# A decoder layer on one core: ScalarE's table set with both logarithm and exponential, read in by the program itself

## What is computed

```python
x = x + attn(layernorm(x))       # 16 heads of 32, windows of 128 stepped by 64
x = x + wkv(w, u, layernorm(x), ctx_2048)
x = x + ffn(layernorm(x))        # 512 -> 2048 -> 512, weights and activations rounded
```

## Time and profile before

| | |
|---|---|
| median of 3 runs | 1103.22 us (1102.84 to 1103.45) |
| the profiled execution, own time | 1107.51 us |
| its span, first to last instruction | 1106.2 us |
| TensorE (PE) busy | 860.3 us, 78% |
| VectorE (DVE) busy | 848.1 us, 77% |
| ScalarE (ACT) busy | 706.9 us, 64% |
| GpSimd (POOL) busy | 436.7 us, 39% |
| mean granted TensorE clock | 0.924 of 2.4 GHz |

### The profile page before, as it was taken

How to read it: one execution, slowest core, us unless ns; L and a number is a source line. 1 busy time by engine, 2 the same in 40 slices (tenths; PEclk the granted TensorE clock), 3 DMA queues, 4 the chain that set the end, 5 groups by cost and what they waited for, 6 DMA issues and landing times.

```text
span 1106.2 us, 21992 instructions
## 1 busy us (share of the span) xinstructions
PE 860.3 (78%) x8301; PEld 512.9 (46%) x8388; DVE 848.1 (77%) x1630; ACT 706.9 (64%) x1179; POOL 436.7 (39%) x495
## 2 busy tenths in 40 slices
PE   5782565768888889897988888888888888986655
PEld 2341444444455555555545555555555554543222
DVE  4552659798888888888888888888788888887953
ACT  0113838077777777777768686868586868594633
POOL 2110113225353535353535354544444444445532
PEclk9896786769999999999999999999999999998978
DMA  8867516011524252525242424243342525122132
GB/s 293 288 217 277 188 58 189 10 59 36 93 68 83 78 83 78 84 78 83 79 83 78 80 82 77 85 75 87 62 99 58 104 58 103 49 78 29 39 58 66
DMA packets 148762, 106.93 MB, mean 97 GB/s; under 512 B 99792, under 2 KB 126128, under 8 KB 147504
## 3 DMA queue, kind: packets, MB, share of 16 engines
q1 hardware_dynamic: 142128, 101.48, 36.2%
q0 software_dynamic: 656, 2.63, 0.7%
q10 hardware_dynamic: 5872, 1.42, 0.6%
HBM read 65.65 MB, written 10.49 MB: 69 GB/s over the span
## 4 chain that ended last, share of the span: by engine, by line
ACT 31%; PE 23%; DVE 18%; issue 15%; DMA 3%; SPq 2%; POOL 1%; DVEq 0%; ACTq 0%; POOLq 0%
PE bank L494 9%; ACT arena L722 6%; PE bank L593 5%; PE bank L513 5%; ACT L774 3%; ACT sums L729 3%; DVE junk L1146 3%; PE bank L583 2%; ACT sums L734 2%; ACT junk L774 2%; ACT junk L779 2%; DVE amax L1112 2%; DVE fs L1155 2%; ACT L745 2%; ACT L722 2%
## 5 line engine op out<-in xcount | busy, mean ns | idle before, releaser
L583 PE MATMUL bank<-w_up_gate,qT 128*128 128x512 bf16 x966 | 232.5, 386 | 48.4 <-ACT junk L774 24.1
L1350 POOL TENSOR_TENSOR work<-junk,lnw 128x512 f32<-128x512 f32 x128 | 188.2, 1490 | 125.1 <-DVE junk L1146 110.7
L1333 POOL TENSOR_TENSOR sums<-sums,blend 128x448 f32<-128x448 f32 x64 | 73.2, 1163 | 270.5 <-ACT sums L734 270.5
L583 PEld LDWEIGHTS bank<-w_up_gate,qT 128*128 128x128 bf16 x1024 | 96.5, 99 | 155.3 <-ACT junk L774 26.9
L593 PE MATMUL bank<-w_down,work 128*128 128x512 bf16 x483 | 125.6, 408 | 25.3 <-ACT junk L774 10.6
L494 PE MATMUL bank<-wide,wq_sb 128*128 128x256 f32 x512 | 117.7, 389 | 27.7 <-DVE rows L1047 27.7
L513 PE MATMUL bank<-wide,k_win 32*128 32x128 f32 x1536 | 70.5, 320 | 82.2 <-ACT arena L722 54.2
L722 ACT ACTIVATE arena<-bank 128x384 f32<-128x384 f32 x256 | 104.8, 496 | 36.7 <-PE bank L513 36.6
L494 PEld LDWEIGHTS bank<-wide,wq_sb 128*128 128x128 f32 x512 | 98.3, 195 | 53.1 <-issue 39.7
L774 ACT ACTIVATE junk<-bank,deq 128x512 f32<-128x512 f32 x128 | 86.3, 686 | 52.5 <-PE bank L583 50.7
L545 PE MATMUL bank<-wo_sb,wide 128*128 128x512 f32 x256 | 115.9, 607 | 4.1 <-DVE wide L1040 4.1
(11 more groups left out here) (150 smaller groups left out, 1541.2 us busy)
## 6 DMA issues: line engine op xcount, KB each, us to landing
rows<-in_x SPq DMA_DIRECT2D x24, 512.0 KB, 5.4
sums<-in_xT SPq DMA_DIRECT2D x16, 512.0 KB, 8.8
wide<-in_xT SPq DMA_DIRECT2D x16, 512.0 KB, 4.2
ctx_T<-in_ctxT SPq DMA_DIRECT2D x16, 512.0 KB, 4.0
wide<-wide SPq DMA_DIRECT2D x64, 128.0 KB, 2.1
out<-rows SPq DMA_DIRECT2D x32, 256.0 KB, 2.2
kv_b<-k_raw SPq DMA_DIRECT2D x16, 384.0 KB
wide<-in_x SPq DMA_DIRECT2D x8, 512.0 KB, 9.3
```

What stands on the lines that cost most here:

```text
L583: last = te.matmul(bank[4 + k % 4][:, :], qT[:, c, t * P:(t + 1) * P], w_up_gate[:, m, c, cols], start=c == 0, stop=c == NC - 1)
L1350: ge.tensor_tensor(hid_w[:, t, cols], hid[:, n % 2, :], lnw[:, cols], op=ALU.mult).then_inc(z_set.sem, 1)
```

## The change

A function `log_tables` is added to ScalarE's stream. It issues one InstLoadActFuncSet for set 6, which holds both Ln and Exp. It is called twice a round where there is a wkv stage (rounds 1 to 16): ahead of `exps(w)` and ahead of `wkv_logs(w, 0)`. The compiler's pass then places no load where the active set already has the function. Nothing else moves, and what is computed stays the same.

```diff
+LN_EXP = 6
...
+        def log_tables():
+            se.add_instruction(mybir.InstLoadActFuncSet(name=nc.get_next_instruction_name(),
+                                                        engine=mybir.EngineType.Activation, act_func_set_id=LN_EXP))
+
...
             if do_w:
+                log_tables()
                 exps(w)
...
             if do_w:
+                log_tables()
                 wkv_logs(w, 0)
```

## The result

| | before | changed |
|---|---|---|
| median of the runs, us | 1103.03 (1102.05 to 1103.45) | 1121.21 (1120.43 to 1122.51) |
| ratio, 95% interval | 1 | 1.0156 [1.0134, 1.0178] |
| profiled execution, us (span) | 1107.51 (1106.2) | 1121.32 (1119.7) |
| loads of a table set | 129 | 84 |
| ScalarE busy, us | 706.9 | 645.9 |

The account below looks back on a forecast made before the run. No engine alone bounds the kernel; the chain goes round between engines (ScalarE 31%, TensorE 23%, VectorE 18%). Steady rounds cost 7.7 + 2.6 = 10.3, i=1 and i=16 give 2.6: 1103.2 + 7.7 = 1111 us, range 1088 to 1117 (own 1103 to 1117).

Parts of the forecast that it names:

- The turns: VectorE and GpSimd instructions on SBUF would meet and wait for each other; L1090 0.7 us late at full clock.
- the tie: First L1040 of VectorE (590.95) against GpSimd's L1370 (590.94); if L1040 wins, the round is 0.0 to 0.1 late, not 0.7.
- A round's price: Full-clock round 0.7 us late if L1370 goes first, 0.0 to 0.1 if L1040 does; with TensorE's clock fallen, 1.1 late.
- Seven rounds with a fall x 1.1 = 7.7: Seven rounds in which TensorE's clock falls to 1.2 GHz for a few microseconds, each 1.1 us late: 7.7 us slower.
- one in every round adds 10: Bound: a fall of TensorE's clock in every round adds 7 x (1.0 + 0.4) = 10 us; given 0.05.
- The first rounds: Round i=1, three loads in its chain: between 0 and 3.9 us off, 2.3 taken.
- The anchor: Profiled execution 1107.51 would take 1115.2; the median of runs is 4.3 below it, so 1103.2 + 7.7 = 1111 us.
- Rival 1: Faster: VectorE-GpSimd meetings cost little and TensorE's 1.3 us gap closes; 1079, or 1092 with half eaten; chance 0.30.
- its point of decision: If a round's last L1040 (VectorE) ends before GpSimd's L1350 behind the third blend starts, the round keeps its lead.
- Rival 2: No difference: the tie goes to VectorE everywhere and clock falls are no more; 1101 to 1105 us; chance 0.14.
- Rival 3: A load costs more than its row by emptying ScalarE: 1.4 us by the rows; 983 us has chance below 0.01.
- Rival 4: The automatic load still follows a set read in by the program, so the time stays as now; chance 0.01.

Follow-up runs that it names:

- experiment 6: Changed kernel with all three removed loads of a round put back where they stood, each loading the set already there: 0.9997 of the kernel before.
- experiment 3: Changed kernel with GpSimd's first product of the second token half (L1359) held for the previous round's quotient, long done: 1.0120 of the kernel before.
- the seventh experiment: Changed kernel with the third load kept (ahead of the exponentials of quarters 2 and 3) and window sums from PSUM: 0.9822 of the kernel before, 1085.78 us.
- the three fillings: 13 idle matmuls in TensorE's waits (1.05, 1.97, 1.3 us), added to kernel before, changed kernel and fastest version: 0.9962, 1.0013, 0.9764 of the kernel before.
- the fourth experiment: Changed kernel with weighted window products left in PSUM and their halves added by one reduce with a single PSUM input: 0.9951 of the kernel before, 1099.21 us.

## Why the prediction was off

The direction and its mechanism were right, the size was not: 1121.2 is 10 above the forecast and 4 above the range.

- **What the loads give.** Right: 84 loads; the third logarithm 2.83 nearer to the second and the exponentials 2.93 (forecast 2.8 and 3.0); TensorE's wait for the Silu gone.
- **The turns.** Right, nearly place by place: the tie went to L1379; L1092 1.62, L1099 1.68 (1.3 to 1.7 were named, but only one of each pair meets, so their medians are 1.16 and 1.18); L1379 1.64; the last L1049 0.94 (0.9 to 1.2); the second L1099 13.08 behind the second logarithm (12.5 to 13.3). The rule that the Trainium skill gives (SBUF — State Buffer, Who interferes with whom) held in its direction in every round read here. An L1049 of 0.36 that lay across a L1359 ended 0.21 behind it, so some 0.15 of it had overlapped; "fully blocks" alone would have given 0.36.
- **A round's price.** At full clock 0.53 against 0.7 (tie lost) or 0.05 (won); I took the middle, 0.37. With a fall 57.7 to 57.9 against 56.7, 1.0 to 1.2, as forecast.
- **The term that was mis-sized: "Seven rounds with a fall x 1.1 = 7.7".** It took the number of falls over from one execution of the kernel before and held it constant under the change; only the price of a turn was added. What the twelve rounds i=3 to 14 hold above twelve full-clock rounds (12 x 55.70 or 12 x 56.23) is the falls' share:

| | rounds with a fall | above full clock, us |
|---|---|---|
| kernel before, first and second profile | 7, 6 | 9.2, 6.6 |
| all loads back (experiment 6) | 5 | 7.4 |
| changed kernel, first and second profile | 7, 9 | 10.9, 15.6 |
| its hold that held nothing (experiment 3) | 7 | 12.4 |

In the first pair of profiles the twelve rounds grew by 8.0 us (685.61 - 677.59), near the forecast (12 of 14 rounds, 8.8). But that execution of the kernel before was 4.3 above its median and held eight falls; the forecast took off the 4.3 and kept the falls. Against the second profile of before (1103.10), the span of the changed kernel's first is 17.9 longer: 6.4 by turns and 4.3 by falls in the twelve rounds, 2.5 in i=2, 3.2 in i=15 (61.38 and 58.69 in its two profiles against 58.15, with three falls in the first and one in the others), 2.0 less in i=1, and 3.6 ahead of i=1 and behind i=15. The fourteen steady rounds so cost 16.3 us where the sum has 10.3. I had "one in every round adds 10" among the bounds and gave it 0.05; some 6 of those 10 came. The runs that filled the pauses show it: without falls in these rounds the two kernels are 5.5 us apart, not 16 to 18.

- **The first rounds.** i=1 came out at -1.7 and -2.6 (66.12 and 65.23 against 67.82; forecast -2.3), but i=2 gave 1.7 and 1.2 back (61.54 and 61.05 against 59.85), with a fall at the transposes (L566), some 37 us behind its exponentials, near the place of the steady rounds' second one.
- **The anchor.** The profiled execution of before holds a round of 58.67 with two falls. The runs of the kernel before on the other chips go from 1101.3 to 1109.6, so 4 us of difference between two of its executions are common; the first ratio (1.0156) is on the high side of the second (1.0136) and third (1.0120).
- **Rival 1** (faster) fell in the changed kernel, but its point of decision was the right one: where the meetings are taken away (the seventh experiment, which also moves the window sums) the round is 54.37, against the 54 to 55 that the prediction gave for that case. Rival 2 fell with the tie, which went to GpSimd, and with the time. Rival 3 fell with the sixth experiment: with the loads back the time is that of the kernel before, 0.9997. Rival 4 fell with the count of 84.

Open: why the falls of the changed kernel come in 7 to 9 rounds and not in all, and why those of the kernel before come in about every second. That the ones at its second place, 34 to 35 us behind the first exponential, stand behind the two waits of TensorE (1.00 and 1.14) is read from its timeline, and that they vanish when pauses are filled is shown, but the three fillings were not tried one by one.

## What to carry to other kernels

Time saved on one engine moves its successors against each other: before an engine's stall is removed, list which two-operand SBUF instructions of VectorE and which of GpSimd will then lie across each other, and consider to keep a cheap wait or to let an operand stay in PSUM. Where rounds come in two kinds by TensorE's clock, count them as a variable of the change, not as a constant: look for pauses of TensorE in front of the falls, and try a dozen idle matmuls in them.

## What the runs showed of the hardware that was not expected

- Twelve matmuls fewer in a round made the kernel 20 us slower (1124.97 against 1105.03), with the granted clock at 0.91 and not 0.98 over the twelve rounds and VectorE's and ScalarE's busy time unchanged. Thirteen useless ones more made it faster, 0.9962.
- A load of 1.28 us a round on ScalarE was worth 18 to 20 us (0.9973 with it, 1.0136 and 1.0156 without), by letting VectorE go first where it meets GpSimd.
- VectorE's instruction that reads a PSUM operand and writes PSUM, and the reduce that reads PSUM alone, were not held up by GpSimd: 0.56 at every place of the fourth experiment's round.
